# The hypergraph layer's mean square by transposing the summed squares, with probabilities turned in place and two pairs of transposed tiles

## What is computed

```python
x = layernorm(x + attention(x, adj))      # weight = adj * exp(q k^T), rows divided by their sum
x = layernorm(x + gcn3(x, adj))           # three times adj @ (x @ W) + b, relu after two of them
x = layernorm(x + hypergraph(x, adj))     # two hypergraph convolutions, see below
x = layernorm(x + mha(x, adj))            # 8 heads, scores times 2 adj, softmax
```

```python
h = relu(hypergraph_conv(x, adj, W1, b1))          # 512 features
mu, var = mean(h), mean(h * h) - mean(h) ** 2
h = (h - mu) * rsqrt(var + 1e-5) * gamma + beta
y = hypergraph_conv(h, adj, W2, b2)
```

## Time and profile before

| | us |
|---|---|
| median of 3 runs | 1071.79 (1071.34 to 1073.0) |
| the profiled execution | 1069.87 |
| its span, first to last instruction | 1068.1 |
| TensorE busy | 1029.0 (96%) |
| VectorE busy | 833.6 (78%) |
| ScalarE busy | 649.7 (61%) |
| GpSimd busy | 480.1 (45%) |
| mean granted clock of TensorE | 0.993 |

### The profile page before, as it was taken

How to read it: one execution, slowest core, us unless ns; L and a number is a source line. 1 busy time by engine, 2 the same in 40 slices (tenths; PEclk the granted TensorE clock), 3 DMA queues, 4 the chain that set the end, 5 groups by cost and what they waited for, 6 DMA issues and landing times.

```text
span 1068.1 us, 21761 instructions
## 1 busy us (share of the span) xinstructions
PE 1029.0 (96%) x8412; PEld 912.8 (85%) x8412; DVE 833.6 (78%) x2216; ACT 649.7 (61%) x1755; POOL 480.1 (45%) x298
## 2 busy tenths in 40 slices
...
DMA packets 17384, 43.35 MB, mean 41 GB/s; under 512 B 2049, under 2 KB 2049, under 8 KB 17153
## 3 DMA queue, kind: packets, MB, share of 16 engines
...
...
## 4 chain that ended last, share of the span: by engine, by line
PE 90%; DVE 5%; ACT 3%; issue 1%; DMA 0%; POOL 0%; POOLq 0%; SPq 0%; DVEq 0%
PE ps L470 82%; PE ps L782 5%; PE ps L723 1%; ACT pr L942 1%; DVE pr L1239 1%; PE ps L573 1%; PE ps L653 1%; DVE x L1124 0%; DVE mx L1244 0%; DMA pr<-in_weights 0%; DVE st L1062 0%; ACT fT_high L879 0%; DVE fT_rest L1142 0%; ACT up_high L919 0%; ACT upT L922 0%
## 5 line engine op out<-in xcount | busy, mean ns | idle before, releaser
L1371 POOL TENSOR_TENSOR pr<-pr,den 128x1024 f32<-128x1024 f32 x64 | 121.6, 1902 | 86.2 <-DVE den L1259 86.0
L942 ACT ACTIVATE pr<-pr,mx 128x128 f32<-128x128 f32 x384 | 149.4, 406 | 9.7 <-DVE mx L1244 9.6
L1325 POOL TENSOR_TENSOR rstd<-var,neg_half 128x4 f32<-128x4 f32 (+1 forms) x84 | 73.3, 873 | 111.6 <-DVE var L1073 110.1
L1078 DVE TENSOR_SCALAR x<-x,mv,rstd 128x256 f32<-128x256 f32 x256 | 91.1, 416 | 34.1 <-POOL rstd L1325 33.9
L1350 POOL TENSOR_TENSOR x<-x,rows 128x1024 f32<-128x1024 f32 x16 | 38.1, 2380 | 170.2 <-PE ps L470 170.2
L1062 DVE BATCH_NORM_STATS2 st<-x 128x6 f32<-128x256 f32 x256 | 92.3, 412 | 1.1
L1239 DVE TENSOR_TENSOR pr<-ps,adjB 128x1024 f32<-128x1024 f32 x64 | 75.2, 1217 | 14.5 <-PE ps L470 14.5
L896 ACT COPY s_s<-ps 128x512 f32<-128x512 f32 x32 | 18.8, 587 | 105.4 <-PE ps L470 105.4
L1360 POOL TENSOR_TENSOR hv<-hv,neg_half 128x2 f32<-128x2 f32 x32 | 22.5, 704 | 129.4 <-DVE hv L1205 129.4
L942 ACT ACTIVATION_READ_ACCUMULATOR pr<-pr,mx 128x1 f32 x384 | 78.7, 205 | 0.0
L1057 DVE TENSOR_TENSOR fT_rest<-ps,fT_high 128x512 fp32r<-128x512 f32 x96 | 62.9, 681 | 20.2 <-ACT fT_high L932 14.4
(11 more groups left out here) (198 smaller groups left out, 3267.4 us busy)
## 6 DMA issues: line engine op xcount, KB each, us to landing
...
```

The source lines that it names most:

```text
L942: act.activation(pr[:, b, k, :], pr[:, b, k, :], ACT.Exp, bias=mx[:, b, k:k + 1], accum_out=den[:, b, 0, k:k + 1]).then_inc(exp_ready, 1)
L1078: dve.tensor_scalar(t[:, b, :], t[:, b, :], mv[i][:, b, 0:1], rstd[i][:, b:b + 1], ALU.subtract, ALU.mult).then_inc(ready, 1)
L1325: pool.tensor_tensor(rstd[i][:, bs], var[i][:, bs], neg_half[:, bs], ALU.pow).then_inc(rstd_ready[i], len(pairs))
L1371: pool.tensor_tensor(pr[:, b], pr[:, b], den[:, b, 1, :].unsqueeze(2).broadcast_to([P, HEADS, P]), ALU.mult).then_inc(pr_ready, 1)
```

## The change

- On TensorE a transpose of sqs for each graph, into 128 columns of the same PSUM bank, takes the place of the one-column matmul. A new step of ScalarE, square_rows, passes each transposed tile through an ACTIVATE in place and sums its rows into the new tile square. VectorE's hyper_down waits for it and takes the factor 1/512 itself; the floor tile is gone.
- prT is gone: the transposed heads are copied back into pr. The constants of the setup that lay in prT lie in x2 and x3.
- axT and z (gcn) get tiles of their own, aT_high and aT_rest. e0 and p0 share one tile.
- All lists are written anew. In the loop: hyper_down0 goes ahead of mha_wo1, gcn_3s1_high ahead of hyper_out, gcn_3s1 and gram_turn behind it; mha_wo0_high ahead of mha_turn2, mha_turn3 between gcn_2s0 and gcn_2s1; on ScalarE mha_exp2b behind the up_out steps and x_split ahead of gcn_2a; on VectorE hyper_rest0 behind both halves of att_out and hyper_y0 ahead of hyper_down1; on GpSimd x0_bias ahead of mha_div2 and x_rest near the end; on SP the load of adjB behind both stores.
- Fillers: the prologue has five in place of six, the epilogue seven in place of four, three of them between the last hyper_out and the last mha_xt.

The lists of the prologue and most of the epilogue are left out here, as are functions in which only fT_rest became aT_rest.

```diff
@@ SCHEDULE (the loop)
         ("C", "mha_qk01"), ("C", "mha_qk01_rest"), ("C", "mha_qk2"), ("C", "mha_qk3"), ("A", "att_v0"),
         ("C", "mha_scores0"), ("A", "att_v1"), ("A", "att_scores"), ("C", "mha_scores1"), ("C", "mha_v0"),
         ("C", "mha_v1"), ("A", "att_turn"), ("B", "hyper_x"), ("A", "att_out"), ("B", "hyper_up01"), ("A", "gram"),
-        ("B", "hyper_up01_rest"), ("B", "hyper_up3"), ("B", "hyper_up2"), ("A", "gcn_ax"), ("C", "mha_turn0"),
-        ("C", "mha_turn1"), ("A", "gcn_1"), ("C", "mha_ctx0"), ("A", "gcn_1_rest"), ("C", "mha_turn2"),
-        ("C", "mha_wo0_high"), ("A", "gcn_2s1_high"), ("A", "gcn_2s0_high"), ("C", "mha_wo0"), ("A", "gcn_2s0"),
-        ("A", "gcn_2s1"), ("C", "mha_turn3"), ("A", "gcn_2a"), ("C", "mha_ctx1"), ("B", "hyper_down0_high"),
-        ("C", "mha_wo1_high"), ("C", "mha_wo1"), ("B", "hyper_down0"), ("B", "hyper_down1_high"),
-        ("B", "hyper_down1"), ("A", "gcn_3s0_high"), ("A", "gcn_3s0"), ("B", "hyper_out"), ("A", "gram_turn"),
-        ("A", "gcn_3s1_high"), ("A", "gcn_3s1")],
-    "DVE": [("B", "gcn_3a0"), ("C", "mha_xt1"), ("C", "mha_xt"), ("B", "gcn_3a1"), ("B", "x1_means0"),
-        ("B", "x1_means1"), ("B", "x1_stats"), ("B", "x1_norm"), ("A", "incidence"), ("C", "mha_scores0"),
-        ("C", "mha_max0"), ("C", "mha_scores1"), ("A", "att_exp"), ("C", "mha_max1"), ("C", "mha_max2"),
-        ("C", "mha_div0"), ("A", "att_out"), ("B", "hyper_rest0"), ("A", "att_res1"), ("B", "hyper_rest1"),
-        ("C", "mha_div1"), ("A", "x0_means0"), ("A", "x0_means1"), ("A", "x0_stats"), ("A", "degrees"),
-        ("C", "mha_max3"), ("A", "x0_norm"), ("C", "mha_shift3"), ("C", "mha_div2"), ("A", "gram_scale"),
-        ("C", "mha_turn1"), ("C", "mha_turn0"), ("A", "gcn_ax"), ("A", "gcn_ax1"), ("C", "mha_sum3"),
-        ("C", "mha_div3"), ("C", "mha_ctx0"), ("A", "z1_rest0"), ("A", "z1_rest1"), ("C", "mha_wo0"),
-        ("C", "mha_turn2"), ("C", "mha_turn3"), ("C", "x3_stats0"), ("C", "mha_ctx1"), ("B", "square_sum0"),
-        ("B", "square_sum1"), ("A", "z2_rest0"), ("C", "mha_wo1"), ("C", "x3_norm0"), ("A", "z2_rest1"),
-        ("B", "hyper_down0"), ("C", "x3_stats1"), ("B", "hyper_down1"), ("B", "hyper_y0"), ("B", "hyper_y1"),
+        ("B", "hyper_up01_rest"), ("B", "hyper_up2"), ("B", "hyper_up3"), ("A", "gcn_ax"), ("C", "mha_turn0"),
+        ("C", "mha_turn1"), ("A", "gcn_1"), ("C", "mha_ctx0"), ("A", "gcn_1_rest"), ("C", "mha_wo0_high"),
+        ("C", "mha_turn2"), ("C", "mha_wo0"), ("A", "gcn_2s0_high"), ("A", "gcn_2s1_high"), ("A", "gcn_2s0"),
+        ("C", "mha_turn3"), ("A", "gcn_2s1"), ("C", "mha_ctx1"), ("A", "gcn_2a"), ("B", "hyper_down0_high"),
+        ("B", "hyper_down0"), ("C", "mha_wo1_high"), ("C", "mha_wo1"), ("B", "hyper_down1_high"),
+        ("B", "hyper_down1"), ("A", "gcn_3s1_high"), ("A", "gcn_3s0_high"), ("A", "gcn_3s0"), ("B", "hyper_out"),
+        ("A", "gcn_3s1"), ("A", "gram_turn")],
+    "DVE": [("B", "gcn_3a0"), ("C", "mha_xt"), ("C", "mha_xt1"), ("B", "gcn_3a1"), ("B", "x1_means0"),
+        ("B", "x1_means1"), ("B", "x1_stats"), ("A", "incidence"), ("B", "x1_norm"), ("C", "mha_scores0"),
+        ("C", "mha_max0"), ("A", "att_exp"), ("C", "mha_scores1"), ("C", "mha_max1"), ("C", "mha_div0"),
+        ("C", "mha_max2"), ("A", "att_out"), ("A", "att_res1"), ("B", "hyper_rest0"), ("C", "mha_div1"),
+        ("B", "hyper_rest1"), ("A", "x0_means1"), ("A", "x0_means0"), ("A", "x0_stats"), ("A", "degrees"),
+        ("C", "mha_max3"), ("A", "x0_norm"), ("C", "mha_shift3"), ("A", "gram_scale"), ("C", "mha_div2"),
+        ("C", "mha_turn1"), ("C", "mha_turn0"), ("A", "gcn_ax"), ("A", "gcn_ax1"), ("C", "mha_ctx0"),
+        ("C", "mha_sum3"), ("C", "mha_div3"), ("A", "z1_rest0"), ("A", "z1_rest1"), ("C", "mha_wo0"),
+        ("C", "mha_turn2"), ("C", "mha_turn3"), ("C", "x3_stats0"), ("B", "square_sum0"), ("C", "x3_norm0"),
+        ("C", "mha_ctx1"), ("B", "square_sum1"), ("A", "z2_rest0"), ("A", "z2_rest1"), ("B", "hyper_down0"),
+        ("C", "mha_wo1"), ("C", "x3_stats1"), ("B", "hyper_y0"), ("B", "hyper_down1"), ("B", "hyper_y1"),
         ("B", "hyper_out"), ("B", "x2_means0"), ("B", "hyper_out1"), ("B", "x2_means1"), ("B", "x2_stats"),
         ("B", "x2_norm"), ("C", "x3_norm1")],
-    "ACT": [("C", "mha_xt"), ("C", "mha_qk01"), ("A", "att_t"), ("C", "mha_qk01_rest"), ("C", "mha_qk2"),
+    "ACT": [("C", "mha_xt"), ("A", "att_t"), ("C", "mha_qk01"), ("C", "mha_qk01_rest"), ("C", "mha_qk2"),
         ("C", "mha_qk3"), ("A", "att_v0"), ("A", "att_v1"), ("A", "att_off"), ("A", "att_exp"), ("C", "mha_exp0a"),
-        ("C", "mha_exp0b"), ("C", "mha_v0"), ("C", "mha_v1"), ("A", "att_turn"), ("C", "mha_exp1b"), ("B", "hyper_x"),
-        ("C", "mha_exp1a"), ("C", "mha_exp2b"), ("C", "mha_exp2a"), ("B", "up_out1"), ("B", "up_out0"),
-        ("B", "up_out3"), ("B", "up_out2"), ("A", "gcn_ax"), ("C", "mha_turn0"), ("C", "mha_turn1"), ("A", "x_split"),
-        ("C", "mha_exp3"), ("C", "mha_ctx0"), ("A", "gcn_1"), ("A", "gcn_2s0"), ("A", "gcn_2s1"), ("C", "mha_turn3"),
-        ("C", "mha_turn2"), ("B", "squares0"), ("C", "mha_ctx1"), ("B", "squares1"), ("A", "gcn_2a"),
-        ("A", "gcn_3s0"), ("A", "gram_turn"), ("A", "gcn_3s1")],
-    "POOL": [("C", "x2_bias"), ("A", "att_t"), ("B", "x1_stats"), ("B", "x1_bias"), ("C", "mha_div0"),
-        ("C", "mha_div1"), ("A", "x0_stats"), ("C", "mha_div2"), ("A", "x_rest"), ("B", "up_rest0"),
-        ("C", "mha_div3"), ("B", "up_rest1"), ("C", "x3_stats0"), ("B", "hyper_down0"), ("B", "hyper_down1"),
-        ("A", "x0_bias"), ("C", "x3_stats1"), ("B", "x2_stats")],
-    "SP": [("B", "gcn_3a1"), ("A", "att_scores"), ("C", "mha_scores1"), ("A", "att_turn"), ("A", "att_out"),
-        ("C", "x3_norm0"), ("C", "x3_norm1")],
+        ("C", "mha_v0"), ("C", "mha_exp0b"), ("C", "mha_v1"), ("A", "att_turn"), ("C", "mha_exp1b"), ("B", "hyper_x"),
+        ("C", "mha_exp1a"), ("C", "mha_exp2a"), ("B", "up_out0"), ("B", "up_out1"), ("B", "up_out2"),
+        ("B", "up_out3"), ("C", "mha_exp2b"), ("A", "gcn_ax"), ("C", "mha_turn0"), ("C", "mha_turn1"),
+        ("C", "mha_exp3"), ("C", "mha_ctx0"), ("A", "gcn_1"), ("C", "mha_turn2"), ("B", "squares0"), ("A", "gcn_2s0"),
+        ("C", "mha_turn3"), ("A", "gcn_2s1"), ("B", "squares1"), ("C", "mha_ctx1"), ("A", "x_split"), ("A", "gcn_2a"),
+        ("B", "square_rows0"), ("B", "square_rows1"), ("A", "gcn_3s0"), ("A", "gcn_3s1"), ("A", "gram_turn")],
+    "POOL": [("C", "x2_bias"), ("A", "att_t"), ("B", "x1_stats"), ("C", "mha_div0"), ("B", "x1_bias"),
+        ("C", "mha_div1"), ("A", "x0_stats"), ("A", "x0_bias"), ("C", "mha_div2"), ("B", "up_rest0"),
+        ("C", "mha_div3"), ("B", "up_rest1"), ("C", "x3_stats0"), ("B", "hyper_down0"), ("A", "x_rest"),
+        ("C", "x3_stats1"), ("B", "hyper_down1"), ("B", "x2_stats")],
+    "SP": [("B", "gcn_3a1"), ("A", "att_scores"), ("A", "att_turn"), ("A", "att_out"), ("C", "x3_norm0"),
+        ("C", "x3_norm1"), ("C", "mha_scores1")],
 }
...
@@ EPILOGUE, "PE"
-        ("gcn_3s1_high", 1), ("hyper_out", 2), ("gcn_3s0_high", 1), ("gcn_3s0", 1), ("gcn_3a0", 1), ("gram_turn", 1),
-        ("hyper_down1", 1), ("hyper_out", 1), ("mha_xt", 1), ("mha_qk01", 1), ("mha_qk01_rest", 1), ("mha_qk2", 1),
...
+        ("hyper_down1", 2), ("hyper_out", 2), ("gcn_3s0_high", 1), ("gcn_3s1_high", 1), ("gram_turn", 1),
+        ("hyper_down1", 1), ("hyper_out", 1), ("keep_busy5", 1), ("keep_busy2", 1), ("keep_busy9", 1), ("mha_xt", 1),
...
-        pr = sb("pr", [P, GB, HEADS, P]); prT = sb("prT", [P, 2, HEADS, P])
+        pr = sb("pr", [P, GB, HEADS, P])
         qkT = sb("qkT", [P, 2 * C, N4]); upT = sb("upT", [P, HC, N4])
...
         s2 = s3 = sb("s2_s3", [P, GB, D])
-        x2T = gxT = axT = z_high = sb("fT_high", [P, C, N4], F32R)
-        fT_rest = sb("fT_rest", [P, C, N4], F32R)
+        axT = z_high = sb("aT_high", [P, C, N4], F32R)
+        x2T = gxT = sb("fT_high", [P, C, N4], F32R)
+        aT_rest = sb("aT_rest", [P, C, N4], F32R); fT_rest = sb("fT_rest", [P, C, N4], F32R)
         xT_high = sb("xT_high", [P, C, N4], F32R); xT_rest = sb("xT_rest", [P, C, N4], F32R)
         off0 = sb("off0", [P, GB]); raw0 = sb("raw0", [P, GB])
-        e0 = sb("e0", [P, GB, P]); p0 = sb("p0", [P, GB, P])
+        e0 = p0 = sb("e0_p0", [P, GB, P])
         p0T = sb("p0T", [P, N4]); rs0 = sb("rs0", [P, GB]); x0 = sb("x0", [P, GB, D])
...
         sqs = sb("sqs", [P, 2, N4])
-        floor = sb("floor", [P, GB, 2]); hv = sb("hv", [P, 4, GB]); y2 = sb("y2", [P, GB, D])
+        square = sb("square", [P, GB]); hv = sb("hv", [P, 4, GB]); y2 = sb("y2", [P, GB, D])
         x2 = sb("x2", [P, GB, D])
         x3 = sb("x3", [P, GB, D])
-        rep = prT[:].rearrange("p t h n -> p (t h) n")
+
+        def rep(k):
+            return (x2, x3)[k // 8][:].rearrange("p b (c n) -> p (b c) n", c=C)[:, k % 8, :]
...
                     for c in range(C):
```

(24 more changed lines are left out.)

62 lines of the change are left out of this document (31 added, 31 removed), and 218 rows, old and new, of tables (EPILOGUE, PROLOGUE).

## The result

The changed kernel takes 1065.17 us (median of four runs, 1063.05 to 1066.17) against 1071.88 before (the 1071.79 above is without its fourth run): ratio 0.9934, 95% interval 0.9919 to 0.995, faster by 0.66%. Run again with five rounds it gave 1064.09 us, 0.9931 (0.9919 to 0.9944). The forecast was 1066.5. The total is right, partly by luck: two of the terms behind it, the order in the loop and the ends, are wrong by 2 to 4 us each, in opposite directions, and the experiments show which.

What follows compares the result with a forecast made beforehand. TensorE's own work was taken to bound the loop. Terms -5.8 + 3.0 + 2.0 + 1.1 - 3.6 - 0.5 - 1.5 = -5.3 took the median 1071.8 to 1066.5 us, range 1060.5 to 1073.5.

Steps and rivals of the forecast that it cites:

- Bound: Inside the loop the time is TensorE's own work in its written order; a gain must shorten distances between its starts.
- Squares, -5.8: TensorE's squares: two transposes replace four one-column instructions at 0.09 us each, saving 0.18 us a half over 32 halves.
- Way to y, +3.0 in the loop: At hyper_out, y is ready at +3.25 us but TensorE asks at +3.03: about 0.25 us wait a pass, 12 passes.
- The skill's estimate: ScalarE's new ACTIVATE, one pointer operand fewer than the exponential, about 93 ns: 0.1 to 0.2 us off the wait.
- +2.0 outside the loop: Longer waits for y in prologue and epilogue, where cover is thinner: together +2.0 us.
- The new order in the loop, -3.6 + 1.1: Two small TensorE waits (gram, mha_turn1) go, 0.3 us a pass; one more matmul-kind switch costs 0.09; 12 passes.
- rival 2: The order gives nothing, other waits of 0.1 to 0.2 us replacing the two removed: 1070.1 us; chance 0.17.
- Ends, -0.5 - 1.5: Prologue with one filler fewer and x0 sooner, -0.5 us; three fillers behind the last hyper_out keep the clock up, -1.5.
- The signs of being wrong: The forecast is wrong if the pass is over 61.8 us or the ends move by more than 3 us.
- (1): Slower: ScalarE's pair of rows is the bound, deciding from 0.32 us on; 1081 us with 1 us more; chance 0.12.
- (3): Two transposes take as long as four one-column matmuls, 0.18 us each: 1072.3 us, no change; chance 0.08.
- (4): Better: no wait at hyper_out and the last stage shorter by 1 to 2 us: 1062 us; chance 0.12.

Runs made afterwards that it cites:

- rows_plus_one: Changed kernel with one more ACTIVATE of the same 128x128 tile on ScalarE between the second half's two rows, output thrown away: 1068.27 us, ratio 0.9976.
- turn_twice: Changed kernel with each transpose of sqs issued twice, four more TensorE instructions a pass: 1069.7 us.
- squares_back: Changed kernel with the old one-column matmuls and hyper_down put back, no rows on ScalarE, new orders and tiles kept: 1065.26 us, ratio 0.9945.
- old_ends: Changed kernel with prologue and epilogue in the order before, ScalarE's rows of squares inserted: 1069.73 us, ratio 0.9989.

## Why the prediction was right, point by point

- **Bound.** TensorE's distances inside the loop: right.
- **Squares, -5.8.** The step held, its size was too small by a fifth. I read 0.09 us an instruction by dividing 0.36 by four. It is 0.11 for both kinds, and each run of them has 0.09 less, from the switch behind it. Eight removed and four added are 0.45 a pass, 0.36 forecast: about -7.2 over 32 halves. The forecast took its price for the transposes from gm's four, and the other row it had, 0.1125, was the right one.
- **Way to y, +3.0 in the loop.** Forecast 0.25 a pass, measured 0.22. Two errors cancel. ScalarE's pair is 0.27 us apart, not 0.39, so VectorE starts y 528.38 - 525.82 = 2.56 us after the transposes instead of 2.77. But TensorE, which by this should have lost next to nothing, loses 0.22: its third product starts at 528.92, 0.12 behind the 527.94 + 0.86 at which it could, and an instruction later another 0.1 is lost. From VectorE's end to TensorE's start my sum had no term. The second 0.1 doesn't depend on the wait: the distance behind a late start is 0.32 us in place of 0.216 where y came 0.28 late (rows_plus_one), 0.11 (the changed kernel) and 0.01 (turn_twice). Why it comes stays open. That the wait is for y, as I put it, is shown by squares_back (0.22) and rows_plus_one (0.17 for 0.16).
- **The skill's estimate.** The new row's ACTIVATE lasts 266 ns on average and the exponential's 407, by the page of the changed kernel. The Trainium skill ("ScalarE: Activation LUTs", What ACT_TABLE_LOAD costs) gave 93 ns for the operand that is gone; the trace agrees in direction, with 141, part of which may be PSUM or the function. Against the attention's exponential, which also reads PSUM and has one such operand (368 ns by the same page), it is 102. The wait did not shrink by it, since VectorE's end to TensorE's start took the time instead.
- **+2.0 outside the loop.** In the first stretch of the epilogue TensorE waits 0.59 + 1.21 = 1.80 us for y; forecast 2.2. In the third group of the prologue the changed kernel loses 0.68 us there against squares_back (from the squares' end through hyper_out 3.73 for 3.05); forecast 0.85. The squares give 1.2 us in all on medians and 2.2 at the same clock, where I had -5.8 + 3.0 + 2.0 = -0.8.

```profile
958.66 1.13 PE L475 MATMUL ps<-y,gmT 128*128 128x256 f32 x4 [0.59 <-DVE y L1233]
961.00 2.08 PE L475 MATMUL ps<-y,gmT 128*128 128x256 f32 x4 [1.21 <-DVE y L1233]
```

- **The new order in the loop, -3.6 + 1.1.** This step failed: it gave 12 x 0.02 = 0.2 us (squares_back), or 0.06 in each pass that lies wholly in the loop, of 0.21 forecast. It is the prediction's rival 2, inside a total that other terms made up. gram's wait for x did go. These are rows of the changed kernel for the earlier trace rows:

```profile
558.15 0.40 PE L475 MATMUL ps<-fT_high,WupT_rest 128*128 128x512 f32 x1
558.39 1.05 PE L475 MATMUL ps<-bhT,hT 128*128 128x129 f32 x8
563.15 1.86 PEld L475 LDWEIGHTS ps<-adjTA,x 128*128 128x128 f32 x16 [0.36 <-DVE x L1089]
556.41 0.19 PEld L475 LDWEIGHTS ps<-fT_high,WupT_high 128*128 128x128 f32 x1 [0.20 <-ACT fT_high L920]
565.04 1.91 PE L787 MATMUL ps<-ident,pr 128*128 128x128 f32 x16
566.88 0.47 PE L475 MATMUL ps<-aT_high,W_high 128*128 128x512 f32 x1
```

  gram starts 0.24 us behind the matmul ahead of it, without a stall. But TensorE then meets VectorE's x0 at gcn_ax (0.36 on the weight load) and, before that, ScalarE's cast at hyper_up01 (0.20). Means over eleven passes, distance to the next step, squares_back against before: att_turn 0.43 for 0.56; att_out 1.70 for 1.55; hyper_up01 to gram 1.98 for 2.23; gram to gcn_ax 4.79 for 4.72; gcn_ax 1.89 for 1.79; mha_turn0 and 1 1.83 for 1.79; from there to the next mha_xt 29.85 for 29.89. The shorter ones make -0.42 together, the longer ones +0.36. That is the 0.06. The second wait that I had removed, mha_turn1's for upT, was none to gain from: upT is ready at 564.74, ahead of the transposes, and 16 of them still take 1.84 us, 0.115 each. 0.09 was again the wrong price.
- **Ends, -0.5 - 1.5.** They gave about -5.6 (old_ends, on medians). The fillers at the end are worth about what I said, 1.9 against 1.5, and the clock was 1.00 from 1020 to 1030 as forecast. Missed were the prologue (0.7 to 2.3 against 0.5) and the second stretch of the epilogue (1.3 against nothing), where I read no row of the new order.
- **Sum.** Forecast: squares -0.8, order in the loop -2.5, ends -2.0. Measured: about -1.2 to -2.2, -0.2 and -5.6. The total was right because the last two missed by 2.3 and 3.6 us in opposite directions, and that is luck.
- **The signs of being wrong.** The pass passed its own (61.53, limit 61.8). The other was that the ends move by more than 3 us: old_ends has them at 5.6, so by it the account of the ends was wrong.
- **Rivals.** (1) fell, but its tipping point was near: rows_plus_one, 0.16 us more, takes 0.17 of the 0.27 that a pass gains, so by extrapolation 0.26 would take it all, where I had 0.32. (3) fell: a transpose costs 0.11, not 0.18. (4) fell: there is a wait.
